# The mixture-of-experts stage rebuilt on token lists: gathers twelve tiles ahead, expert weights transposed during the relative attention, and the norm of three sequences within its last rounds

## The reference, cut to what matters

```python
h = _layernorm(x) * (1 + ca) + sa
x = x + ga * relative_attention(h)       # 16 heads of 8, softmax over 512 keys, tables rel_k, rel_v
h = _layernorm(x) * (1 + cb) + sb
# experts: E = 8, D = 128, HD = 512
expert_ids = argmax(softmax(h @ router_w.T))            # one expert for each token
u = square(relu(h @ expert_fc[e]))                      # (.., 512)
out = u @ expert_proj[e].T                              # (.., 128), of the token's expert e alone
x = x + gb * out                                        # gb: one row of 128 for each sequence
```

## Time and profile before

| what | us |
|---|---|
| median of three runs | 2559.96 |
| the profiled execution, its own time | 2556.95 |
| its span, first to last instruction | 2555.2 |
| relative attention's rounds, first scores to the meeting | 1904.9 to 2414.9 |
| experts, from the meeting to the end | 2414.9 to 2555.2 |
| busy over the span: PE, DVE, ACT, POOL | 2367.3, 1749.7, 1600.4, 1477.4 |

### The profile page before, as it was taken

The page is one execution under the profiler, slowest core; times in us unless marked ns, Lnnn a source line. Parts: engine busy times, 40 slices in busy tenths (PEclk is TensorE's granted clock), DMA queues, the critical chain, the costliest instruction groups (busy, mean ns, idle before and its releaser), DMA issues.

```text
span 2555.2 us, 121984 instructions
## 1 busy us (share of the span) xinstructions
PE 2367.3 (93%) x53661; PEld 1739.5 (68%) x53661; DVE 1749.7 (68%) x3521; ACT 1600.4 (63%) x5055; POOL 1477.4 (58%) x1452
## 2 busy tenths in 40 slices
PE   9858999999999999999999999999889999999855
PEld 8736777777777777777777777777546666666654
DVE  4497887888878888888888877887345555555422
ACT  3226777777777777777777777777534454454322
POOL 1156676666766676667766676664137665566144
PEclk9979999999999999999999999999979999999967
DMA  4013333333333334333343333333132222222255
GB/s 90 14 32 81 80 83 95 91 82 83 94 90 88 85 83 95 93 85 83 93 95 80 86 91 80 89 85 85 36 78 51 47 47 47 48 47 47 69 193 166
DMA packets 234111, 203.55 MB, mean 80 GB/s; under 512 B 133720, under 2 KB 160230, under 8 KB 233454
## 3 DMA queue, kind: packets, MB, share of 16 engines
q1 hardware_dynamic: 227070, 181.28, 29.2%
q0 software_dynamic: 4336, 14.16, 1.7%
q10 hardware_dynamic: 2176, 0.33, 0.1%
HBM read 84.09 MB, written 16.15 MB: 39 GB/s over the span
## 4 chain that ended last, share of the span: by engine, by line
PE 68%; DVE 16%; issue 5%; POOL 3%; SPq 3%; DMA 3%; ACT 2%; POOLq 0%; ACTq 0%; DVEq 0%
PE psum L1197 8%; PE psum L1215 5%; PE psum L1223 5%; PE psum L1899 5%; PE psum L1098 5%; PE psum L1878 4%; PE psum L1884 3%; PE psum L1100 3%; PE psum L1099 3%; PE psum L1931 3%; DVE kT L1430 3%; PE psum L1921 3%; DVE rotated L1405 3%; PE psum L1174 2%; PE psum L1205 2%
## 5 line engine op out<-in xcount | busy, mean ns | idle before, releaser
L1342 ACT ACTIVATE p<-p,stat 128x64 f32<-128x64 f32 x1536 | 512.3, 336 | 38.2 <-DVE stat L1477 36.2
L1560 POOL TENSOR_TENSOR p<-p,inverse 128x512 f32<-128x512 f32 x192 | 200.3, 1043 | 461.6 <-DVE inverse L1480 460.4
L1197 PE MATMUL psum<-kT,qT 32*32 32x64 f32 x24576 | 305.5, 223 | 27.3 <-issue 25.9
L1197 PEld LDWEIGHTS psum<-kT,qT 32*32 32x32 f32 x24576 | 263.5, 103 | 78.1 <-issue 76.8
L2028 DVE TENSOR_REDUCE largest<-psum 128x1 f32<-128x512 f32 x256 | 164.9, 686 | 221.5 <-PE psum L1884 221.5
L1405 DVE SCALAR_TENSOR_TENSOR rotated<-psum,scales,rotary 128x512 f32<-128x512 f32 x384 | 271.5, 742 | 26.3 <-ACT sq L1278 26.0
L1342 ACT ACTIVATION_READ_ACCUMULATOR p<-p,stat 128x1 f32 x1536 | 289.1, 188 | 0.0
L1539 POOL TENSOR_TENSOR sq<-sq 128x512 f32<-128x512 f32 x192 | 245.3, 1277 | 46.6 <-ACT sq L1278 46.5
L1278 ACT ACTIVATE sq<-psum 128x512 f32<-128x512 f32 x384 | 213.0, 582 | 68.6 <-PE psum L1128 52.3
L1952 ACT ACTIVATE w_by_key<-psum 128x512 f32<-128x512 f32 x128 | 76.5, 597 | 245.0 <-PE psum L1899 245.0
L1215 PEld LDWEIGHTS psum<-pT,v_win 64*64 64x64 f32 x12288 | 197.0, 135 | 48.0 <-issue 40.7
(11 more groups left out here) (344 smaller groups left out, 5488.2 us busy)
## 6 DMA issues: line engine op xcount, KB each, us to landing
v_win<-v_tok SPq DMA_DIRECT2D x576, 128.0 KB
rnorm_wide<-rnorms SPq DMA_DIRECT2D x384, 64.0 KB
v_win<-v_tok SPq DMA_DIRECT2D x336, 64.0 KB
...
```

The costliest lines, as they stand in the source:

```text
L1197: last = PE.e.matmul(psum[WIN * blk:WIN * (blk + 1), f, out], q[rows, g, half, tok:tok + WIN], k[rows, g, half, tok:tok + 2 * WIN], start= ...
L1342: last = A.e.activation(p, p, ACT.Exp, bias=t.stat[:, h, 2 * g + f:2 * g + f + 1], accum_out=t.sum[:, h, g, f:f + 1])
L1560: G.e.tensor_tensor(p, p, t.inv[:, h, :, :].unsqueeze(3).to_broadcast([P, GROUPS_TF, 2, 2 * WIN]), ALU.mult).then_inc(*t.p_scaled.by(m))
```

## The change: what it does

- `hT`, `xc`, the router's tensors and the table become tensors of the whole program. `hT` and `xc` share memory with a query buffer of block 0.
- The table is built during the relative attention. SP issues the copy of expert_fc before round 0, loads expert_proj e in round e+1 and stores it transposed in round e+6. PE transposes it in round e+4, between the softmax weights and the values; ACT copies it in the same round, ahead of its own copy of the softmax weights. The router is transposed in round 12.
- The norm of sequences 0 to 2 is made in rounds 129 (centering, squares), 131 (sums), 132 (1/std) and 134 (spreading, scaling). The experts' phase makes that of sequence 3 alone.
- Scatter, reload, answers' store and final gather go. h, x and the gate are stored as DRAM rows of 3x128 numbers, one for each token, and a row of zeros for no token. DVE and PE turn the places into a list: for each tile and place the number of the token, or 2048 for none. POOL gathers each tile's 128 rows of 1.5 KB by that list, 12 tiles ahead, and scatters each tile's finished output rows straight to the output; numbers of 2048 are dropped.
- A tile's weights are one 128 by 1024 block of the table, which SP loads with an address read from memory into a register, 10 ahead. DVE multiplies by the gate and adds x in each tile.

```diff
+    c.wide = sbuf(c, whole, "wide", [P, 2 * B, S])
+    c.hT, c.xc = c.wide[:, 0:B, :], c.wide[:, B:2 * B, :]
...
+    c.table = nc.dram_tensor("expert_table", (NE * P, 2 * HD), F32, kind="Internal").ap()
...
-    norm_signals(c, (0, 2, 3))
+    norm_signals(c, {0: [B - 1], 2: [B - 1], 3: [B - 2, B - 1]})
+    c.norm3 = Norm(c, 3, c.hT, c.xT, c.xc, c.modT[:, 1, 4, :], c.modT[:, 1, 3, :])
...
+TABLE_FIRST, TABLE_FETCH, TABLE_LAG = 4, 3, 2
+ROUTER_AT = TABLE_FIRST + NE
+EARLY_FIRST = ROUNDS_UNIT * len(UNITS) + 1
+EARLY_AT = {"center": 0, "square": 0, "sum": 2, "root": 3, "spread": 5, "scale": 5}
...
+def fetch_weights(c, t, e):
+    SP = c.SP
+    SP.wait_ge(*c.norms["normed"].on((2, B - 1)))
+    if e >= 4:
+        SP.wait_ge(*t.pr_turned.on(e - 4))
+    SP.e.dma_start(t.xc[:, e % 4, :], c.io["L1_ffn_expert_proj"][e]).then_inc(*t.pr_in[e % 4].by(e))
+def store_weights(c, t, e):
+    SP = c.SP
+    SP.wait_ge(*t.pr_kept.on(e))
+    SP.e.dma_start(c.table[e * P:(e + 1) * P, HD:2 * HD], t.hT[:, e % 4, :]).then_inc(*t.pr_out[e % 4].by(e))
+def turn_weights_down(c, t, e):
+    PE = c.PE
+    PE.wait_ge(*t.v_kept.all())
+    PE.wait_ge(*t.pr_in[e % 4].on(e))
+    if e:
+        PE.wait_ge(*t.pr_kept.on(e - 1))
+    for j in range(TPB):
+        last = PE.e.transpose(c.psum[:, 7, j * P:(j + 1) * P], t.xc[:, e % 4, j * P:(j + 1) * P], c.ident[:, :])
+    last.then_inc(*t.pr_turned.by(e))
+def keep_weights_down(c, t, e):
+    A = c.A
+    A.wait_ge(*t.projected.on((B - 1, "v")))
+    A.wait_ge(*t.pr_turned.on(e))
+    if e >= 4:
+        A.wait_ge(*t.pr_out[e % 4].on(e - 4))
+    A.e.activation(t.hT[:, e % 4, :], c.psum[:, 7, :], ACT.Copy).then_inc(*t.pr_kept.by(e))
+def turn_router(c, t):
+    PE = c.PE
+    PE.wait_ge(*t.router_in.all())
+    PE.wait_ge(*t.pr_kept.all())
+    PE.e.transpose(c.psum[:, 7, 0:NE], c.rw[:, :], c.ident[0:NE, 0:NE]).then_inc(*t.rw_turned.by(0))
+def early_norm_tensor(c, t, s):
+    PE = c.PE
+    for b in range(B - 1):
+        if s == EARLY_AT["center"]:
+            norm_center_tensor(c, c.norm3, b)
+        if s == EARLY_AT["sum"]:
+            norm_sum_tensor(c, c.norm3, b, t.e[b], B - 1)
+        if s == EARLY_AT["spread"]:
+            norm_spread_tensor(c, c.norm3, b)
+def early_norm_scalar(c, t, s):
+    if s == EARLY_AT["square"]:
+        for b in range(B - 1):
+            norm_square_scalar(c, c.norm3, b, t.e[b])
+def early_norm_vector(c, t, s):
+    if s == EARLY_AT["root"]:
+        norm_root_vector(c, c.norm3, 0, B - 2, B - 1)
+    if s == EARLY_AT["scale"]:
+        for signal in t.pr_out:
+            c.V.wait_ge(*signal.all())
+        for b in range(B - 1):
+            norm_scale_one(c, c.norm3, b)
...
 def relative_sync(c, t):
     SP = c.SP
+    for i, (to, name) in enumerate(((c.rw[:, :], "L1_ffn_router_w"), (c.order[:, :], "c_first"))):
+        SP.e.dma_start(to, c.io[name]).then_inc(*t.router_in.by(i))
+    SP.e.dma_start(c.upper[:, :], c.io["c_upper"][:, 0, :]).then_inc(*t.router_in.by(2))
+    SP.e.dma_start(c.table[:, 0:HD], c.io["L1_ffn_expert_fc"].rearrange("e d h -> (e d) h")).then_inc(*t.fc_in.by(0))
     for r, at, valued in relative_rounds():
+        if 0 <= r - TABLE_FIRST + TABLE_FETCH < NE:
+            fetch_weights(c, t, r - TABLE_FIRST + TABLE_FETCH)
+        if 0 <= r - TABLE_FIRST - TABLE_LAG < NE:
+            store_weights(c, t, r - TABLE_FIRST - TABLE_LAG)
...
-    for signal in (*t.qd_in, *t.o_out.values(), *t.o_in.values()):
+    for signal in (*t.qd_in, *t.o_out.values(), *t.o_in.values(), t.fc_in, *t.pr_out):
...
+        if 0 <= r - TABLE_FIRST < NE:
+            turn_weights_down(c, t, r - TABLE_FIRST)
+        if r == ROUTER_AT:
+            turn_router(c, t)
...
-                PE.wait_ge(*t.v_kept.all())
+                PE.wait_ge(*t.rw_kept.on(0))
...
+        early_norm_tensor(c, t, r - EARLY_FIRST)
...
 def relative_keep(c, t, n):
...
+        if 0 <= r - TABLE_FIRST < NE:
+            keep_weights_down(c, t, r - TABLE_FIRST)
+        early_norm_scalar(c, t, r - EARLY_FIRST)
...
@@ relative_vector
+        if r == ROUTER_AT:
+            V.wait_ge(*t.rw_turned.on(0))
+            V.e.tensor_copy(c.rwT[:, :], psum[:, 7, 0:NE]).then_inc(*t.rw_kept.by(0))
+        early_norm_vector(c, t, r - EARLY_FIRST)
...
@@ experts_setup
-WEIGHTS, UP_LAG, DOWN_LAG = 6, 1, 3
+WEIGHTS, LOOK, UP_LAG, DOWN_LAG = 10, 12, 1, 3
+NO_TOKEN = NT * P
...
+    t.rows = dram("token_rows", (NT * P + 1, 3 * P))
...
@@ experts_sync
+    SP.wait_ge(*t.none_set.on(0))
+    SP.e.dma_start(t.rows[NO_TOKEN:NO_TOKEN + 1, :], t.none[:, :]).then_inc(*t.rows_out.by("none"))
+    part = lambda b, j: t.rows[b * S:(b + 1) * S, j * P:(j + 1) * P].rearrange("(k p) d -> p k d", p=P)
+    SP.wait_ge(*t.gate_kept.on(0))
+    for b in range(B):
+        SP.e.dma_start(part(b, 2), t.gates[:, b:b + 1, :].to_broadcast([P, TPB, P])).then_inc(*t.rows_out.by(("g", b)))
+    stores = [(*h, b) for h in (("h", t.h_kept, t.htok, 0), ("x", t.x_kept, t.xtok, 1)) for b in range(B - 1)]
+    for name, kept, source, j, b in (*stores, ("h", t.h_kept, t.htok, 0, B - 1), ("x", t.x_kept, t.xtok, 1, B - 1)):
+        SP.wait_ge(*kept.on(b))
+        SP.e.dma_start(part(b, j), source[:, b * TPB:(b + 1) * TPB, :]).then_inc(*t.rows_out.by((name, b)))
+    SP.wait_ge(*t.rowed.on(0))
     for n in range(TILES):
-        SP.wait_ge(*t.y_kept.on(n))
-        SP.e.dma_start(t.answers[n * P:(n + 1) * P, :], t.y[n % 4][:, :]).then_inc(*t.y_out[n % 4].by(n))
-    out = io["out"].rearrange("b (c p) d -> p (b c) d", p=P)
-    for b in range(B):
-        SP.wait_ge(*t.added.on(b))
-        SP.e.dma_start(out[:, b * TPB:(b + 1) * TPB, :], t.ytok[:, b * TPB:(b + 1) * TPB, :]).then_inc(*t.stored.by(b))
+        row = SP.e.value_load(t.row_i[0:1, n:n + 1], min_val=0, max_val=(NE - 1) * P)
+        if n >= WEIGHTS:
+            SP.wait_ge(*t.downed.on(n - WEIGHTS))
+        SP.e.dma_start(t.w[n % WEIGHTS][:, :], c.table[bass.ds(row, P), :]).then_inc(*t.w_in[n % WEIGHTS].by(n))
     SP.wait_ge(*t.stored.all())
...
@@ experts_tensor
+    norm_center_tensor(c, c.norm3, B - 1)
+    turn_tokens(c, t, t.hT, 0, t.h_turned)
+    turn_tokens(c, t, t.hT, 1, t.h_turned)
+    norm_sum_tensor(c, c.norm3, B - 1, c.sq4[B - 1], 6)
+    turn_tokens(c, t, t.hT, 2, t.h_turned)
+    for b in range(B - 1):
+        logits_tensor(c, t, b)
+    norm_spread_tensor(c, c.norm3, B - 1)
+    for b in range(B - 1):
+        turn_tokens(c, t, c.xT, b, t.x_turned)
+    PE.wait_ge(*c.norms["normed"].on((3, B - 1)))
+    logits_tensor(c, t, B - 1).then_inc(*t.logits_out.by(0))
+    turn_tokens(c, t, t.hT, B - 1, t.h_turned)
+    counts_tensor(c, t)
+    PE.wait_ge(*t.h_kept.on(B - 1))
+    turn_tokens(c, t, c.xT, B - 1, t.x_turned)
+    list_tensor(c, t)
     PE.wait_ge(*t.x_kept.all())
-    PE.wait_ge(*t.placed.on(0))
...
+            PE.wait_ge(*t.xs_in[r % (LOOK + 1)].on(r))
+            PE.e.transpose(psum[:, r % 2, 0:P], t.xs[:, r, 0:P], c.ident[:, :]).then_inc(*t.turned.by(r))
...
-                PE.wait_ge(*t.y_kept.on(n - 2))
+                PE.wait_ge(*t.gated.on(n - 2))
...
+def turn_tokens(c, t, source, b, turned):
+    for k in range(TPB):
+        last = c.PE.e.transpose(c.psum[:, b, k * P:(k + 1) * P], source[:, b, k * P:(k + 1) * P], c.ident[:, :])
+    last.then_inc(*turned.by(b))
...
+def list_tensor(c, t):
+    PE, lists = c.PE, c.psum[:, 6, 0:2 * TILES]
+    PE.wait_ge(*t.placed.on(0))
+    for m in range(NT):
+        last = PE.e.matmul(lists, t.in_slot[:, m, :], t.ids[:, m, :, :].rearrange("p j t -> p (j t)"), start=(m == 0), stop=(m == NT - 1))
+    last.then_inc(*t.listed.by(0))
...
@@ experts_vector
+    norm_root_vector(c, c.norm3, B - 1, B - 1)
+    norm_scale_one(c, c.norm3, B - 1)
...
+    for r in range(TILES + DOWN_LAG - UP_LAG):
+        n = r
+        if n < TILES:
+            V.wait_ge(*t.upped.on(n))
+            if n >= 3:
+                V.wait_ge(*t.squared.on(n - 3))
+            V.e.tensor_scalar(t.relu[n % 3][:, :], psum[:, 2 + n % 2, :], 0.0, None, ALU.max).then_inc(*t.relued.by(n))
+        n = r - DOWN_LAG + UP_LAG
+        if n >= 0:
+            V.wait_ge(*t.downed.on(n))
+            V.e.tensor_tensor(t.y[:, n, :], psum[:, 4 + n % 2, 0:P], t.xs[:, n, 2 * P:3 * P], ALU.mult).then_inc(*t.gated.by(n))
+            V.wait_ge(*t.gated.on(n))
+            V.e.tensor_tensor(t.y[:, n, :], t.y[:, n, :], t.xs[:, n, P:2 * P], ALU.add).then_inc(*t.added.by(n))
...
@@ places_vector
+    tiles = [P, TILES, NE]
+    then(V.e.tensor_tensor(t.past[:, :, :], t.tile_n[:, :].unsqueeze(2).to_broadcast(tiles), t.end[:, :].unsqueeze(1).to_broadcast(tiles), ALU.is_ge))
+    then(V.e.tensor_reduce(t.expert[:, :], t.past[:, :, :], AX, ALU.add))
+    V.e.tensor_scalar(t.row_i[:, :], t.expert[:, :], float(NE - 1), float(P), ALU.min, ALU.mult).then_inc(*t.rowed.by(0))
...
-    V.e.tensor_copy(t.at_i[:, :], t.at[:, :]).then_inc(*t.placed.by(0))
+    then(V.e.tensor_copy(t.at_i[:, :], t.at[:, :]))
```

(67 more changed lines are left out.)

206 lines of the change are left out of this document (66 added, 140 removed).

## The result

The changed kernel took 2544.98 us (2544.22 to 2554.62, five runs) beside 2561.9 us (2552.66 to 2569.27) of the kernel before on the same chip: ratio 0.9943, 95% interval 0.992 to 0.9965. It is faster, by 0.6%, where I had forecast 1.4%; it lies above my range. Its profiled execution took 2544.75, span 2542.9, against a sum of 2521.5.

What follows compares the result with a forecast made beforehand. PE was taken to bound the attention rounds, a different engine each stage of the experts' phase. 6.6 + 7.9 - 49.9 = -35.4 against 2556.95 gave 2521.5; median put at 2523, own range 2513 to 2533.

Steps and rivals of the forecast that it cites:

- A: Attention rounds 4 to 11: transposing expert weights there costs +6.6 us; bounds +0.7 to +17.
- Rival 1: Rounds: the moved work costs nothing, A and B at zero, 14.5 us less, 2508; chance 0.08.
- B: Attention rounds 129 to 134: the early norm's PE work is paid, not hidden, +7.9 us; bounds 0 and 15.8.
- C, list: Experts' phase: token list ready 27.4 us after the meeting, first gather at 28.3; bounds 3 us earlier or 4 later.
- rival 5: Start of the tile loop: gathers land behind 5 MB of weights, first tile about 36, not 33; 2523 stays.
- C, the step that failed: Tile loop: PE does 23 tiles in 50 us beside POOL's 46 transfers, whose last starts at 87.3 us.
- POOL waiting for `added`: Tile loop: a sign named beforehand that the prediction is wrong; outputs were expected 7 us before their scatter's turn.
- C, the tail: End of experts' phase: last scatter lands 2.25 us after its start, closing takes 0.8, end at 90.4.
- the spacing: POOL's 46 transfers in the experts' phase: starts 1.31 us apart, 45 x 1.31 from 28.3 to 87.3.
- Rival 2: Tile loop: POOL's transfers slow down beside DVE's additions; 23 at +0.5 give +12, 2535, all 46 +23; chance 0.11.
- Rival 3: Clock in the rounds: PE's idling lowers it, A = 17 and B = 15.8, +18, 2541; chance 0.10.
- Rival 4: Tile loop: SP's weight loads with addresses from memory are slow; over 4.3 us each makes the kernel slower; chance 0.04.

Runs made afterwards that it cites:

- z1: The changed kernel itself, nothing edited, run on chip 4 beside a kernel with 22 gathers ahead: 2519.77 us, ratio 0.9881 to the kernel before.

## Why the prediction missed, step by step

- **A, +6.6:** measured +6.0. The step 1.34 to 2.84 us was 2.76, and the eighth transposes came 4.60 us behind the seventh instead of 5.86, with no wait for POOL. Right. Rival 1 falls.
- **B, +7.9:** +9.7. The mechanism was right (the norm's PE work is paid in full), the size was short by 1.8, and the granted clock of 0.81 in that stretch lies in it; it stayed inside the bound of 15.8. A + B = 15.7 against 14.5, and the rounds from the zeroed sums to the phase, 545.0 against 529.6, say 15.4.
- **C, list:** ready 27.3 us after the meeting (27.4 forecast), first gather at 28.2 (28.3). First tile at 35.0, not 33: the rows landed behind the weights at a DMA share of 1.00, as in rival 5, and as there it decided nothing.
- **C, the step that failed:** "PE beside it: first tile at about 33, 23 tiles in 50 us with ramp and waits", with POOL's row of 46 transfers ending last. The tile loop took 66.9 us from first tile to last answer, and POOL waited 18.0 us for answers. The last scatter started at 103.7 instead of 87.3: +16.4. Nothing in the trace of before contained this wait: POOL ran there with about 1 us idle between its transfers while PE worked (18.67 busy of 50), and the same holds no longer in the new loop (32.07 of 51). I had costed only POOL's side of a row without gaps, and put nothing for what that row would do to PE's results. The prediction's own sign of being wrong, POOL waiting for `added`, came true; its transfers, at 1.04 and 1.02 us, were as priced.
- **C, the tail:** from the last scatter's start to the end 5.1 us, not 3.05: +2.0. I took the landing of a scatter into DRAM of before (2.25) and 0.8 for closing; that sum was short.
- **Where the profiled 2544.75 comes from:** 2521.5, +3.8 for a later start of the rounds (the memset of L1746 at 1889.5, against 1885.7 before), +0.9 in the rounds, +16.4 and +2.0 in the phase: 2544.6. The 3.8 are no part of the change: the same code came there between 1873.8 and 1889.5 in the profiles of this study.

```profile
L1746 DVE MEMSET psum<- x1: 485/485/485, 1889.5 to 1889.5; 128x512 f32 x1
```

- **Where the loop is not late** the prediction's terms can be tried against z1 on chip 4. Its list was ready at 29.6 us of the phase, the 45 spacings took 60.2 us (1.337, forecast 1.31), then 5.1: with 0.9 for the first start, 95.7 us. From the meeting, 0.4 earlier, that is 96.1 against 90.4: +2.5 for the list, +1.2 for the spacing, +2.0 for the tail. Its time, 2519.8, is near 2523 partly by luck: those 5.7 us stand against rounds that started 7.3 earlier than in the profile of before. The ratio, 0.9881, has the forecast's 2523/2559.96 = 0.9856 just inside its interval.
- **Rival 2** (transfers slower beside DVE's additions) and the rule behind it: in z1 all 23 additions fell among POOL's transfers, whose medians are 1.04 and 1.01 us and whose slowest scatter took 1.13. The Trainium skill, SBUF — State Buffer, "Who interferes with whom", has a DVE instruction with two SBUF inputs contend with POOL's reads of SBUF. The prediction worked out 7 us from that. The same passage goes on to say that a probe of DMA stalls saw `tensor_copy` cause them and `tensor_tensor` not; these additions are `tensor_tensor`, and the trace agrees with it: it shows no slower transfer.
- **Rival 3** (clock) needed A = 17 and B = 15.8; they measured 6.0 and 9.7. The loop's 0.86 stands beside stalls; z1's loop without them had 0.95, as the loop before. **Rival 4** (slow weight loads by SP) falls with 0.34 us for an issue.

What is shown: on chip 1, in one execution of each kernel, opening 1.1 us between gathers removes the lateness, and taking the traffic away does not; five kernels without such gaps all had it there. What is not: which part of the chip delays PE's results, why chip 4 with the same program, and chips 9 and 10 with its variants, show none, on which kind of chip the first profile was taken (its lateness of 21.7 is like the 19.1 on chip 1), and whether it is POOL's idle time or the lower rate of gathers that helps. A complete kernel with gaps was not run: POOL's row would be 18 x 0.81 = 15 us longer (an estimate), which costs about as much as the lateness.
